# The middle of a written-out batch pipeline put into a loop that runs on the chip

## The reference

```
q, k, v = split(x @ c_attn_w + c_attn_b)
attn = softmax(causal(q k^T / sqrt(8)))          # heads 0 to 2: columns reweighted, rows normalised again
x = layernorm(x + (attn v) @ c_proj_w + c_proj_b)
h = relu(s0 * [x, -x] @ (+-1 matrix k0)) * 2      # 256 -> 512
h = relu(s1 * h @ (+-1 matrix k1)) * 2            # 512 -> 512
x = layernorm(x + s2 * h @ (+-1 matrix k2))       # 512 -> 128
```

## Time and profile before

| | us |
|---|---|
| median of 3 runs | 1005.2 |
| lowest, highest | 1003.4, 1006.76 |
| the profiled execution | 1005.2 |
| its span in the trace | 1003.3 |
| TensorE busy | 901.3 (90%) |
| VectorE busy | 671.5 (67%) |
| ScalarE busy | 604.2 (60%) |
| GpSimd busy | 438.2 (44%) |

### The profile page before, as it was taken

The page is one execution under the profiler, slowest core; times in us unless marked ns, Lnnn a source line. Parts: engine busy times, 40 slices in busy tenths (PEclk is TensorE's granted clock), DMA queues, the critical chain, the costliest instruction groups (busy, mean ns, idle before and its releaser), DMA issues.

```text
span 1003.3 us, 18215 instructions
## 1 busy us (share of the span) xinstructions
PE 901.3 (90%) x6848; PEld 502.5 (50%) x6848; DVE 671.5 (67%) x1752; ACT 604.2 (60%) x1106; POOL 438.2 (44%) x505
## 2 busy tenths in 40 slices
PE   2349799999999999999999999999999999999866
PEld 1125344555555554555555554655565554645343
DVE  2255668586877868586877868585867869685334
ACT  2105557576666757576766757576766767476733
POOL 1102334545454554545454554535554554435430
PEclk9657999999999999999999999999999999999887
DMA  3654545345353535445353525454353525300000
GB/s 77 67 68 60 66 54 65 53 61 68 42 68 41 74 39 75 52 63 67 44 66 42 75 40 75 50 65 65 49 64 43 73 30 75 39 23 2 23 10 10
DMA packets 66141, 53.23 MB, mean 53 GB/s; under 512 B 4519, under 2 KB 64007, under 8 KB 66055
## 3 DMA queue, kind: packets, MB, share of 16 engines
q1 hardware_dynamic: 65190, 51.30, 40.2%
q10 hardware_dynamic: 864, 0.79, 0.3%
HBM read 9.24 MB, written 4.19 MB: 13 GB/s over the span
## 4 chain that ended last, share of the span: by engine, by line
PE 63%; ACT 18%; DVE 7%; DMA 5%; issue 2%; SPq 2%; POOL 1%; ACTq 1%; POOLq 0%; DVEq 0%
PE av_ps L875 11%; PE max_ps L816 10%; PE score_ps L842 10%; PE bank_ps L902 7%; PE bank_ps L903 7%; ACT e L513 6%; PE bank_ps L799 4%; ACT res L531 4%; PE max_ps L818 4%; PE bank_ps L948 3%; DVE h_hi L717 3%; ACT full L505 2%; DMA stack<-negmaxT 2%; DMA stack<-parts 2%; PE bank_ps L937 2%
## 5 line engine op out<-in xcount | busy, mean ns | idle before, releaser
L513 ACT ACTIVATE e<-score_ps 128x512 f32<-128x512 f32 x640 | 370.5, 597 | 210.4 <-PE score_ps L842 207.6
L816 PE MATMUL max_ps<-stack 72*128 72x512 bf16 (+3 forms) x1024 | 277.6, 311 | 31.4 <-DMA stack<-parts 24.1
L842 PE MATMUL score_ps<-stack 75*128 75x512 bf16 (+3 forms) x1024 | 247.1, 303 | 24.5 <-DMA stack<-negmaxT 16.7
L638 DVE TENSOR_REDUCE negmax<-max_ps 128x1 f32<-128x512 f32 x256 | 170.2, 684 | 127.9 <-PE max_ps L818 127.6
L422 POOL TENSOR_SCALAR_AFFINE_SELECT e<-e 128x512 f32<-128x512 f32 x256 | 162.8, 656 | 139.2 <-ACT e L513 139.2
L429 POOL TENSOR_TENSOR h_lo<-full,h_hi 128x512 fp32r<-128x512 f32 x120 | 155.1, 1297 | 112.4 <-DVE h_hi L717 112.4
L816 PEld LDWEIGHTS max_ps<-stack 72*128 72x128 bf16 x1024 | 101.8, 99 | 192.0 <-issue 73.4
L818 PE MATMUL max_ps<-ident_bf,future_bf 128*128 128x128 bf16 x1024 | 197.4, 224 | 0.0
L875 PE MATMUL av_ps<-e,vaug 128*9 128x512 f32 (+3 forms) x2048 | 187.4, 438 | 2.1 <-ACT avT L520 1.9
L641 DVE TENSOR_REDUCE negmax<-max_ps 128x1 f32<-128x384 f32 x256 | 140.3, 548 | 47.4 <-PE max_ps L818 47.0
L505 ACT ACTIVATE full<-bank_ps,scales 128x512 f32<-128x512 f32 x128 | 86.6, 688 | 99.9 <-PE bank_ps L903 97.0
(11 more groups left out here) (86 smaller groups left out, 945.8 us busy)
## 6 DMA issues: line engine op xcount, KB each, us to landing
stack<-parts SPq DMA_DIRECT2D x288, 128.0 KB
x_in<-in_L_attn_hidden_states SPq DMA_DIRECT2D x16, 256.0 KB, 4.8
x_res<-in_L_attn_hidden_states SPq DMA_DIRECT2D x16, 256.0 KB, 11.0
out_x<-res SPq DMA_DIRECT2D x16, 256.0 KB, 10.3
stack<-negmaxT ACTq DMA_DIRECT2D x32, 24.0 KB
e<-in_L_ffn_k SPq DMA_DIRECT2D x1, 256.0 KB, 3.1
wc<-in_L_attn_c_attn_w SPq DMA_DIRECT2D x1, 192.0 KB
e<-in_L_ffn_k SPq DMA_DIRECT2D x1, 128.0 KB, 3.2
```

The costliest lines, as they stand in the source:

```text
L513: nc.scalar.activation(e[g % 2][:, t, :], score_ps[:, t % 2, :], ACT.Exp, scale=SCALE).then_inc(exped, 1)
L638: ins = nc.vector.reduce_max(negmax[:, half, 3, h + t:h + t + 1], buf, AX.X, negate=True)
L816: nc.tensor.matmul(out_ap[:, col:col + width], st[0:QK_ROWS, h, 0, P * qt:P * qt + P], st[0:QK_ROWS, h, 1, 0:width], start=True, stop=False)
L842: return nc.tensor.matmul(out_ap[:, col:col + width], st[0:ALL_ROWS, h, 1, P * kt:P * kt + P], st[0:ALL_ROWS, h, 0, P * kt:S], start=True, ...
```

## The change

`run` now writes out iterations -2, -1, 0, 1 and 2, then opens a loop that the engine itself counts (`eng.Fori`) with a body of two iterations (`UNROLL = 2`) and five trips, for the iterations 3 to 12, and then writes out 13 to 17. Each of the five engines has its own such loop, with its own counter; nothing makes the engines meet at its ends. An `At` in the loop carries the counter's register, and each number that depends on it becomes an expression of the register: `exped >= reg * 80 + 40 c + ...`. So every wait in the body compares a semaphore with a register, which has to be computed, and the DRAM addresses of `x` and `out` on SP do too. Buffers are still chosen by the parity of a constant, since the body holds an even number of iterations. The engine instructions, their order and what they wait for stay the same. `apart` puts one empty instruction between a wait and what follows at five places: two on SP, the `mask` of POOL, `layernorm_var` on DVE.

```diff
+UNROLL = 2
 class At:
-    def __init__(self, c):
-        self.c = c
+    def __init__(self, c, reg=None):
+        self.c, self.reg = c, reg
     def times(self, per, plus=0):
-        return self.c * per + plus
+        k = self.c * per + plus
+        return k if self.reg is None else self.reg * (UNROLL * per) + k
     def of_parity(self, per, plus=0):
-        return self.c // 2 * per + plus
+        k = self.c // 2 * per + plus
+        return k if self.reg is None else self.reg * per + k
...
+    LOOP = (3, B - 3)
...
-        i = used_before[n.c] + sum(0 <= n.c + d < B for d in before)
-        return i % 2, i // 2 + 1
+        if n.reg is None:
+            i = used_before[n.c] + sum(0 <= n.c + d < B for d in before)
+            return i % 2, i // 2 + 1
+        i = used_before[LOOP[0]] + USES * (n.c - LOOP[0]) + len(before)
+        return i % 2, n.reg * (UNROLL * USES // 2) + (i // 2 + 1)
...
-        def run(iteration):
-            for n in range(FIRST, LAST + 1):
+        def run(eng, iteration):
+            for n in range(FIRST, LOOP[0]):
+                iteration(At(n))
+            with eng.Fori(0, (LOOP[1] - LOOP[0]) // UNROLL) as i:
+                for u in range(UNROLL):
+                    iteration(At(LOOP[0] + u, i))
+            for n in range(LOOP[1], LAST + 1):
                 iteration(At(n))
...
+        def apart(eng):
+            eng.nop(nofuse=True)
...
                 sp.wait_ge(split_step, b.times(3, 3))
+                apart(sp)
                 if live(n + -1):
                     sp.wait_ge(scored, (n + -1).times(G * STEPS, 4 * STEPS))
...
                 pool.wait_ge(exped, n.times(G * STEPS, STEPS * g + after))
+                apart(pool)
...
                 dve.wait_ge(ln_step[i], b.times(4, 1))
+                apart(dve)
...
-            run(iteration)
+            run(pe, iteration)
```

More of the change, by code:

```diff
@@ L125, in block_kernel @@
     FIRST, LAST = -2, B + 1
-    assert (D, H, T, FT, R) == (128, 16, 4, 4, 8)
+    LOOP = (3, B - 3)
+    assert (D, H, T, FT, R) == (128, 16, 4, 4, 8) and (LOOP[1] - LOOP[0]) % UNROLL == 0
     def live(b):
-        return 0 <= b.c < B
+        return b.reg is not None or 0 <= b.c < B
+    USES = len(BANK_USES)
     used_before = {FIRST: 0}
@@ L133, in block_kernel @@
         used_before[n + 1] = used_before[n] + sum(0 <= n + d < B for _, d in BANK_USES)
+    assert used_before[LOOP[1]] - used_before[LOOP[0]] == USES * (LOOP[1] - LOOP[0]) and UNROLL % 2 == 0
     def use(n, what):
         before = [d for w, d in BANK_USES[:[w for w, _ in BANK_USES].index(what)]]
[L138 to L139 removed]
+        if n.reg is None:
[3 more added lines that the diff above has]
+        return i % 2, n.reg * (UNROLL * USES // 2) + (i // 2 + 1)
     def use_of(b, what):
@@ L267, in last_batch @@
         def last_batch(b):
-            return b.c == B - 1
+            return b.reg is None and b.c == B - 1
         def full_slot(b, k):
@@ L318, in later_half @@
                 b = n + 1
-                if not live(b) or (b.c == 0):
+                if not live(b) or (b.reg is None and b.c == 0):
                     return
                 sp.wait_ge(split_step, b.times(3, 3))
+                apart(sp)
                 if live(n + -1):
@@ L329, in earlier_half @@
                     return
-                if b.c == 0:
+                if b.reg is None and b.c == 0:
                     wait_free(sp, use_of(b, "q"))
@@ L355, in iteration @@
                 if live(n):
-                    if n.c > 0:
+                    if n.c > 0 or n.reg is not None:
                         wait_free(sp, use_of(n + -1, "proj"))
                     sp.dma_start(x_res[:], x_tok[n.times(1)]).then_inc(xres_loaded, 16)
-            run(iteration)
+            run(sp, iteration)
             sp.wait_ge(stored, 16 * B)
@@ L454, in split_qk @@
                     b = n + 2
-                    if live(b) and not (b.c == 0):
+                    if live(b) and not (b.reg is None and b.c == 0):
                         split(b, k)
@@ L493, in _ @@
             pool.wait_ge(w_loaded, 16 * 8)
-            run(iteration)
+            run(pool, iteration)
         @block.scalar
@@ L508, in exp @@
                 act.wait_ge(scored, n.times(G * STEPS, STEPS * g + t + 1))
-                if n.c == 0 and g == 0 and t == 0:
+                if n.reg is None and n.c == 0 and g == 0 and t == 0:
                     act.wait_ge(setup_step, 8)
-                if t == 0 and not (n.c * G + g < 2):
+                if t == 0 and not (n.reg is None and n.c * G + g < 2):
                     act.wait_ge(summed, n.times(G, g - 1))
@@ L517, in sums_out @@
                 act.wait_ge(summed, b.times(G, g + 1))
-                if g == 0 and b.c > 0:
+                if g == 0 and (b.reg is not None or b.c > 0):
                     wait_full(act, use_of(b + -1, "tok_3"))
@@ L522, in activation_out @@
             def activation_out(b, k, what, func, **kw):
-                if b.c * 9 + k >= 2:
+                if b.reg is not None or b.c * 9 + k >= 2:
                     act.wait_ge(split_ready, b.times(9, k - 1))
@@ L572, in iteration @@
                                 i = "qk".index(what)
-                                if i == 0 and b.c > 0:
+                                if i == 0 and (b.reg is not None or b.c > 0):
                                     act.wait_ge(split_step, b.times(3))
-                                if i == 0 and b.c > 1:
+                                if i == 0 and (b.reg is not None or b.c > 1):
                                     for half in range(2):
@@ L593, in iteration @@
                             nc.scalar.activation(parts[n.parity][:, 1:5:3, :], qk[:], ACT.Copy).then_inc(split_step, 1)
-            run(iteration)
+            run(act, iteration)
         @block.vector
@@ L669, in take_negmaxT @@
                 wait_full(dve, u)
-                if b.c > 0:
+                if b.reg is not None or b.c > 0:
                     dve.wait_ge(negmax_in[half], b.times(16))
@@ L678, in take_v @@
                 va = vaug[b.parity]
-                if b.c > 1:
+                if b.reg is not None or b.c > 1:
                     dve.wait_ge(summed, b.times(G, -G))
@@ L779, in iteration @@
                             layernorm_var(n + -2, 1)
-            run(iteration)
+            run(dve, iteration)
         @block.tensor
@@ L810, in max_scores @@
                     last_use = max(j - G * STEPS for j in range(G * STEPS) if j % MAX_RING == i)
-                if not (b.c == 0 and last_use < 0):
+                if not (b.reg is None and b.c == 0 and last_use < 0):
                     pe.wait_ge(max_taken, b.times(G * STEPS, last_use + 1))
@@ L831, in scores @@
                 st, out_ap = stack[n.parity], score_ps[:, t % 2, :]
-                if t == 0 and g == 0 and n.c == 0:
+                if t == 0 and g == 0 and n.reg is None and n.c == 0:
                     pe.wait_ge(ones_in[0], 16)
@@ L836, in scores @@
                     pe.wait_ge(negmax_in[g // 2], n.times(16, 16))
-                if not (n.c == 0 and g == 0 and t < 2):
+                if not (n.reg is None and n.c == 0 and g == 0 and t < 2):
                     pe.wait_ge(exped, n.times(G * STEPS, STEPS * g + t - 1))
@@ L859, in sums @@
                         pe.wait_ge(v_ready, b.times(1, 1))
-                    if not (b.c == 0 and g == 0):
+                    if not (b.reg is None and b.c == 0 and g == 0):
                         pe.wait_ge(av_out, b.times(G, g))
@@ L967, in fill_bank @@
                     m = int(what[5])
-                    if m == 0 and b.c == 0:
+                    if m == 0 and b.reg is None and b.c == 0:
                         pe.wait_ge(setup_step, 8)
```

4 lines of the change are left out of this document (2 added, 2 removed).

## The result

The changed kernel took 1046.56 us (median of 4 runs, 1042.14 to 1053.75), the kernel before 1005.98 (4 runs, 1003.4 to 1009.23): a ratio of 1.041, with a 95% interval of 1.034 to 1.048. The forecast was 1012 us, with 1027 as the upper end of its range. The profiled execution took 1043.98 us.

What follows compares the result with a forecast made beforehand. The prediction took TensorE, busy 901.3 of 1003.3 us, to bound the kernel. It added 4 us for four jumps back and 3 us for register work to 1005.2 us, giving 1012 us, range 1004 to 1027.

Steps and rivals of the forecast that it cites:

- 4 x 1.0 us: Four jumps back, after iterations 4, 6, 8, 10: 1.0 us each, 4 us in all, bounds 0 and 15 us.
- 4 x 3.7 = 15 us: Upper bound for the four jumps back: no reading ahead, TensorE 3.7 us late at each, all on the path.
- DVE's fetch: At a jump back, 2.7 + 0.5 = 3.2 us; DVE 2.5 us late without reading ahead, maxima ring three banks deep.
- other traffic adds little: At the jumps, DMA engines 0.22 then 0.09 busy just before the boundary; under load a fetch could be 4.8 us.
- Reading ahead: At the jumps, sequencers ahead of their engines hide fetches: 4 us of it makes an edge 0; 1.0 us taken.
- TensorE stands still at each jump: Rival at the jumps back: 3.7 us an edge, 15 us, with 3 us of registers 1023 us; chance 0.16.
- All is covered: Rival: reading ahead or a body still on chip hides fetches, register work fits between; 1 us, 1006 us; chance 0.33.
- faster: Rival: shifted waits win a few tenths of TensorE's 1.6 us idle an iteration; 1001 us at best; chance 0.03.
- Register work binds: Rival in loop iterations: register operations set TensorE's pace; at 150 ns each, 61 us an iteration, +50 us, 1055; chance 0.06.
- TensorE's fetch: At a jump back, 2.7 + 1.2 = 3.9 us for the instructions at the branch target.
- The register term: Waits computed from the counter in the loop: 0.3 us an iteration, 3 us in ten iterations.
- the signature: Expected trace: under 87 packets, about 7 TensorE packets again per trip, gaps near 342, 454, 567, 680 us.

Runs made afterwards that it cites:

- e4: Changed kernel with SP starting the later half's nine `stack` DMAs ten steps into the new iteration: 1145.87 us, ratio 1.138.
- e10: Changed kernel with SP starting the later half's nine `stack` DMAs three steps into the new iteration: 1027.12 us, ratio 1.023.
- e2: Changed kernel with only DVE looping, the other four engines written out: 1047.31 us, ratio 1.041.
- e3: Changed kernel with the first instruction of DVE's loop at the start of an instruction block: 1026.8 us, ratio 1.020.
- e9: Kernel before, no loop, TensorE stopped at the ends of iterations 4, 6, 8, 10 for two successive tiny DMAs: 1023.18 us, ratio 1.018.
- e1: Changed kernel with DVE's ten middle iterations written out, the other four engines looping: 1027.28 us, ratio 1.020.
- e6: Changed kernel with TensorE written out and DVE's loop starting at an instruction block, four engines looping: 1006.27 us, ratio 1.001.
- e7: Changed kernel with `UNROLL = 10`: one trip, no jump back, no registers in waits, `apart` kept: 1004.61 us, ratio 1.000.
- e8: Kernel before, no loop, TensorE stopped at the ends of iterations 4, 6, 8, 10 for one tiny DMA: 1007.96 us, ratio 1.004.
- e5: Changed kernel with a prefetch hint for the jump back at each trip's head, on TensorE and DVE: 1013.31 us, ratio 1.005.
- e11: Changed kernel with the jump hint on TensorE only and DVE's loop starting at an instruction block: 1012.04 us, ratio 1.007.

## Why the prediction was wrong

**The step that failed** is the term "4 x 1.0 us" for the jumps back. The four cost 38.8 us, 9.7 each (after); even the upper bound, 4 x 3.7 = 15 us, was too low by more than half. Three things were wrong in it.

- *DVE's fetch.* It was put at 3.2 us, since "other traffic adds little": the earlier trace rows end at 456 us. But the earlier trace rows have the nine `stack` DMAs issued from 454.31 on, for 5.95 us, just when DVE fetches. The prediction used that row only for SP's slack. The quiet price was about right (2.8 us, e4 and e10); the real one was 6.0 to 8.5, and TensorE waited 0.5 to 4.0 us more for DVE behind its own stop. e2 shows it to be enough for the whole loss, and e3 that without it 20 us are gone.
- *Reading ahead.* I took it to cover most of a fetch. At the first jump TensorE's branch was read at 341.7 with work in hand until 343.0, so 1.3 us of 3.5 were covered; DVE's at 344.4 with work until 345.1, 0.7 of 8.5. The pace of the burst in the earlier trace rows shows that a sequencer can be fast, not that it is far ahead.
- *The clock.* The sum had no term for it, as the earlier trace rows show 1.00. A stop of 2 us by itself brings 3.4 us at the lower level and costs 3.4 in all (e9). Of TensorE's stops at the jumps in e1, e3 and e10 the eight of 2.1 to 2.6 us brought 10.2 us of it each and cost 6.6 to 6.9; the four of 2.65 to 2.93 us brought 3.4, 3.4, 6.8 and none. DVE's stop keeps TensorE idle for 7.6 to 7.9 us, brings 10.2 us of it and costs 10.3 (e2).

**The rivals.** "TensorE stands still at each jump" had the right mechanism for TensorE at 3.7 us an edge: its stop was shorter, 2.2 to 2.8 us in e1, and the clock made 6.8 of it. That DVE's stop could be the longer was in none of them; the prediction had it 2.5 us late behind three banks. "All is covered" and "faster" fell with the first jump. "Register work binds" fell too: between jumps the intervals are at most 0.2 us longer.

**What held.** TensorE's fetch was put at 3.9 us and takes 3.5 to 3.8 (3.3 to 4.1 in the other runs). That an edge costs the largest of the stops, not the sum, held: 10.3 with both (after), 10.3 with DVE's alone (e2). The register term, 0.3 us an iteration, was too large: 56.4 for 56.3, so 1 us rather than 3, though an operation on a register takes 32 to 40 ns in the trace (`ALU_OP` records of the loop), inside the 21 to 88 assumed. SP, POOL and the empty instructions of `apart` cost 0 (e6, e7). ACT was expected to fetch and be 2.0 us late; it fetched nothing. Most of the signature was right: gaps before the first `max_scores` and `take_max` at 342, then every two iterations, with about seven packets of TensorE's queue again for each trip (nine were). Its fewer than 87 packets in all was wrong: there were 103. It also said what would refute it, a gap of over 4 us, and it came to 7.88.

**The rule weighed.** In the changed kernel TensorE stops at a taken branch for 3.5 us and more and DVE for 6.0 and more; ACT, POOL and SP, whose bodies have 299, 142 and 73 instructions, are through in 0.3 us. The Trainium skill, "Runtime: NRT & Kernel Launch", section on instruction fetch mechanics, has a taken branch stall until its page has come if the target is outside the current two-page window: the first two agree with it, and the other three pay nothing at jumps that go back over 299, 142 and 73 instructions, nor does DVE over its 355 once its loop begins at a block's start (e3).

**Open.** Why the clock stays low 10.2 us after stops of 2.1 to 2.6 us and for less after slightly longer ones (e10 has two of each, and behind the fourth jump of e1 it does not fall at all). What decides whether DVE's body stays on chip, beyond where it begins. Why the fourth jump of the changed kernel cost DVE 6.0 us and not 8.3, with as much DMA traffic.

## What to carry to other kernels

A loop on the chip is free for an engine whose body stays on chip, and costs a fetch at each jump for one whose body doesn't: look at the instruction packets and the time behind each branch, engine by engine, and keep the bound engine written out, or hint it and pay once at the exit. Price the fetch with the DMAs that start at that same place, not with those that ended before it. A stop of a bound TensorE can cost more than its length, if its clock falls afterwards: one of 2.0 us cost 3.4 (e9), one of 0.76 us cost 0.6 (e8).

## What the runs showed of the hardware that was not expected

- An instruction fetch waits behind data DMAs: on DVE it took 2.8 us with the DMA engines 0.03 to 0.04 busy and its packet started 1.0 us after the jump (e10); it took 6.0 to 8.5 us with them 0.56 to 0.57 busy and the packet started 3.6 to 5.8 us after (after).
- A loop body of 355 instructions on DVE was read again each trip, with its first instruction at a block's start never (e3); one of 299 on ACT never in any case.
- TensorE's body, some 1,900 instructions, was read again each trip without a hint (64 packets in all) and never with one (28).
- A hint costs on the way out: an interval of 62.2 us in place of 56.5, once. The code behind the loop was asked for only when TensorE had stopped (e5, e11).
- A stop of 0.76 us left TensorE's clock at 1.00; stops of 2.0 us brought 0.50 for 3.4 us, eight of 2.1 to 2.6 us for 10.2 us, four of 2.65 to 2.93 us for 0 to 6.8 us.
